# Five-stage software pipeline over 16 groups: every engine walks the groups in flight in another order

## Reference

```
# layer 0
x  = x + tanh(g_xattn[0]) * performer(q=LN(x), k=ctx, v=ctx)  # exp features, 16 heads of 8, causal prefix sums, num/den
x  = x + tanh(g_ffn[0])   * (sigmoid(xr @ Wr.T) * (relu(xk @ Wk.T)**2 @ Wv.T))   # xr, xk: mix of LN(x) and its previous row
# layer 1
x  = x + tanh(g_xattn[1]) * proj(att_w * softmax(S2) @ v + (1 - att_w) * softmax(q k.T) @ v)   # S2 from a gated softmax
x  = x + tanh(g_ffn[1])   * bitlinear(silu(bitlinear(LN(x), w_gate)) * bitlinear(LN(x), w_up), w_down)  # 8-bit rows, 3-level weights
```

## Time and profile before

| | us |
|---|---|
| median of 3 runs | 536.93 (536.85 to 537.79) |
| the profiled execution, its own time | 536.82 |
| its span in the trace | 535.0 |
| PE busy | 445.9 (83%) |
| DVE busy | 415.1 (78%) |
| ACT busy | 372.3 (70%) |
| POOL busy | 300.7 (56%) |

### The profile page before, as it was taken

How to read it: one execution, slowest core, us unless ns; L and a number is a source line. 1 busy time by engine, 2 the same in 40 slices (tenths; PEclk the granted TensorE clock), 3 DMA queues, 4 the chain that set the end, 5 groups by cost and what they waited for, 6 DMA issues and landing times.

```text
span 535.0 us, 18867 instructions
## 1 busy us (share of the span) xinstructions
PE 445.9 (83%) x7511; PEld 335.3 (63%) x7540; DVE 415.1 (78%) x1372; ACT 372.3 (70%) x769; POOL 300.7 (56%) x415
## 2 busy tenths in 40 slices
PE   0467588989999999999999999999999999877632
PEld 0355456767676767676868676767676767554521
DVE  3521368498989898998989898989898989898634
ACT  1423646587878787978787878787878787776532
POOL 4322035556666667575848584848485766563620
PEclk9999999899999999999999999999999999989765
DMA  7601010100101010101010101101010100000000
GB/s 169 146 2 37 6 32 11 34 9 2 46 10 45 9 45 10 43 12 42 11 42 13 40 15 29 26 20 35 10 42 3 50 4 22 2 21 12 2 10 11
DMA packets 35109, 15.14 MB, mean 28 GB/s; under 512 B 12496, under 2 KB 34896, under 8 KB 35024
## 3 DMA queue, kind: packets, MB, share of 16 engines
q1 hardware_dynamic: 32528, 12.79, 9.6%
q10 hardware_dynamic: 2496, 1.14, 0.9%
HBM read 9.73 MB, written 2.10 MB: 22 GB/s over the span
## 4 chain that ended last, share of the span: by engine, by line
PE 61%; ACT 13%; DVE 9%; POOL 8%; issue 5%; SPq 3%; DMA 1%; POOLq 0%
PE TP L1430 10%; PE MC L1463 8%; PE FP L1338 7%; PE MA L1354 6%; PE FP L1317 4%; POOL ft L385 3%; ACT ft L594 3%; ACT ft L595 3%; PE FP L1321 3%; PE FP L1319 3%; PE SP L1421 2%; ACT E L631 2%; PE SP L1534 2%; DVE WT L941 2%; PE FP L1280 2%
## 5 line engine op out<-in xcount | busy, mean ns | idle before, releaser
L1463 PEld LDWEIGHTS MC<-Vc,ET 128*64 128x64 f32 x2048 | 66.8, 140 | 28.0 <-issue 26.2
L385 POOL TENSOR_SCALAR ft<-ft 128x512 f32<-128x512 f32 x64 | 39.5, 617 | 74.2 <-ACT ft L595 70.6
L1463 PE MATMUL MC<-Vc,ET 128*64 128x25 f32 x2048 | 73.1, 220 | 3.2 <-ACT ET L636 2.3
L408 POOL TENSOR_TENSOR Zn<-E,rsh 128x1024 f32<-128x1024 f32 x32 | 60.9, 1902 | 11.3 <-DVE rsh L1001 11.1
L416 POOL TENSOR_TENSOR Zn<-Zn,Gs 128x1024 f32<-128x1024 f32 x32 | 60.8, 1902 | 3.1 <-DVE Gs L1012 1.6
L642 ACT ACTIVATE ET<-TP 128x512 f32<-128x512 f32 x64 | 38.0, 596 | 27.3 <-PE TP L1430 27.3
L941 DVE TENSOR_TENSOR WT<-FP,mask 128x512 f32<-128x512 f32 x64 | 43.4, 680 | 15.7 <-PE FP L1338 15.6
L1338 PE MATMUL FP<-ft 32*64 32x64 f32 x2048 | 39.6, 228 | 15.3 <-POOL ft L385 10.5
L1338 PEld LDWEIGHTS FP<-ft 32*64 32x64 f32 x2048 | 35.9, 141 | 23.3 <-issue 18.3
L981 DVE TENSOR_REDUCE mx<-SP 128x16 f32<-128x1024 f32 x32 | 39.0, 1219 | 6.6 <-PE SP L1421 6.5
L636 ACT ACTIVATE ET<-TP 128x512 f32<-128x512 f32 x64 | 38.0, 597 | 7.2 <-PE TP L1430 6.3
(11 more groups left out here) (195 smaller groups left out, 1158.4 us busy)
## 6 DMA issues: line engine op xcount, KB each, us to landing
Cd<-in_ctx SPq DMA_DIRECT2D x32, 128.0 KB, 2.9
kX<-kT SPq DMA_DIRECT2D x256, 8.0 KB
X<-in_x SPq DMA_DIRECT2D x16, 128.0 KB, 2.3
call<-in_ctx SPq DMA_DIRECT2D x4, 512.0 KB, 9.5
out_x<-X SPq DMA_DIRECT2D x16, 128.0 KB, 1.9
wffn<-in_L_ffn_w_gate ACTq DMA_DIRECT2D x1, 256.0 KB, 4.3
wffn<-in_L_ffn_w_up ACTq DMA_DIRECT2D x1, 256.0 KB, 4.7
wffn<-in_L_ffn_w_down ACTq DMA_DIRECT2D x1, 256.0 KB, 6.7
```

The costliest lines, as they stand in the source:

```text
L385: pool.tensor_scalar(f, f, EPS_K, 1.0, ALU.add, ALU.mult).then_inc(s("ftp"), 1)
L408: pool.tensor_tensor(z, E1[u][:, :].rearrange("p (h m) -> p h m", m=64), rsh[u][:, :].unsqueeze(2).to_broadcast([P, H, 64]), ALU.subtract) ...
L1463: last = mm(MC[64 * j:64 * j + 64, c + 32 * q:c + 32 * q + 25], weights[:, q, 64 * j:64 * j + 64], Vc[g.p][:, 2 * u + j, q, 0:25], start=T ...
```

## The change

No operation, buffer, bank or setup routine is added or removed. The order of the calls in `step` changes on POOL, ACT, DVE and PE, and waits are added or dropped where the new order asks for it. Some operations also move over a step's border: `least(c,0)`, `shift(c,0)`, `shifted(c,0)`, `ftp(a,1)`, `yD(d)` and `gates_mean(a)` are now at the end of the step before, `token_mix(c)` now stands at the start of the step after.

POOL's whole list, and the two helpers of DVE whose waits changed:

```diff
             def step(a, b, c, d, e):
-                if b:
-                    ftp(b, 1)
-                if d:
-                    shifted(d, 0)
                 if e:
                     quant_int(e)
+                if d:
+                    scaled(d, 0)
+                    shifted(d, 1)
+                    scaled(d, 1)
                 if c:
                     add_X2(c)
-                if d:
-                    scaled(d, 0)
                 if a:
                     veA(a)
+                    rsA(a)
...
+                if a:
+                    ftp(a, 1)
+                if c:
+                    shifted(c, 0)
...
             def gated_G(g, u):
 
-                if u == 0:
-                    at(v, s("r1"), g.k * 2 + 1)
+                at(v, s("r1"), g.k * 2 + 1 + u)
                 v.tensor_tensor(Gs[u][:, :], gate[g.p][:, u, :], rs1[u][:, :], ALU.mult).then_inc(s("Gs"), 1)
 
             def first(g, u):
 
-                if u == 1:
-                    at(v, s("r1"), g.k * 2 + 2)
                 v.scalar_tensor_tensor(n1[u][:, :, :], heads(MC[:, 0:256])[:, :, 0:8], wmix[:, 1:2],
```

More of the change, by code:

```diff
@@ L1124, in step @@
                 if d:
-                    shift(d, 1)
-                if c:
-                    ffn0(c)
+                    gated(d, 0)
+                    gated_G(d, 0)
+                    first(d, 0)
                 if b:
@@ L1130, in step @@
                 if d:
-                    gated_G(d, 0)
-                    first(d, 0)
+                    least(d, 1)
+                if e:
+                    quant_kh(e)
+                if d:
+                    shift(d, 1)
+                    gated(d, 1)
+                    gated_G(d, 1)
+                    first(d, 1)
                 if a:
                     stA(a)
-                if c:
-                    stC(c)
+                if e:
+                    ffn_h(e, 0)
+                    ffn_hu(e, 0)
                 if a:
@@ L1151, in step @@
                 if e:
-                    ffn_h(e, 0)
-                if d:
-                    gated(d, 1)
+                    ffn_hrec(e, 0)
+                    ffn_hs(e, 0)
+                if b:
+                    attend0(b)
                 if e:
[L1156 to L1161, removed]
+                    ffn_h(e, 1)
                 if c:
@@ L1214, in step @@
                     gates(a)
+                    gates_mean(a)
+                if d:
+                    stD(d)
+                    mvD(d)
+                if e:
+                    ffn_out(e, 0)
+                if c:
+                    least(c, 0)
+                if d:
+                    nbD(d)
                 if c:
@@ L1563, in step @@
             def step(a, b, c, d, e):
-                if d:
-                    outA(d, 0)
-                if c:
-                    ffn0_in(c)
                 if b:
@@ L1570, in step @@
                 if d:
+                    outA(d, 0)
                     turn1(d, 2)
+                    turn1(d, 3)
+                if c:
+                    ffn0_in(c)
+                if e:
+                    ffn_in(e)
+                if d:
+                    outA(d, 1)
+                if e:
+                    ffn_gu(e, 0)
+                if d:
+                    turn2(d, 0)
+                    turn2(d, 1)
+                if b:
+                    weights0(b, 1)
                 if c:
@@ L1574, in step @@
                 if d:
-                    turn1(d, 3)
+                    outB(d, 0)
                 if e:
-                    ffn_in(e)
-                if c:
-                    gates_bc(c)
-                if b:
-                    weights0(b, 1)
-                if e:
-                    ffn_gu(e, 0)
-                if d:
-                    outA(d, 1)
-                    turn2(d, 0)
+                    ffn_gu(e, 1)
                 if b:
@@ L1638, in step @@
                     features(a, 1)
+                if c:
+                    scores(c, 1)
+                    turn1(c, 0)
+                if e:
+                    ffn_dn(e, 1)
+                if b:
+                    rows_BT(b)
+                if c:
+                    turn1(c, 1)
             run(pe, step, late)
```

234 lines of the change are left out of this document (90 added, 144 removed).

## The result

The kernel after takes 538.42 us (median of 20 runs, 536.90 to 540.98), the kernel before on the same chip 536.87 us (20 runs, 534.40 to 538.98). The ratio is 1.0036, its 95% interval 1.0020 to 1.0052: slower by 0.36%. Forecast were 538.7 us and slower. The profiled execution took 539.44 us, with a span of 537.7.

What follows compares the result with a forecast made beforehand. PE was taken to set the pace, DVE close behind. 109.2 before the full steps, 337.8 for twelve of 28.15 and 89.9 behind make 536.9 us of span, with 1.8 around it 538.7; range 523 to 552, this case alone 533 to 545.

Steps and rivals of the forecast that it cites:

- The hold: Full step, DVE: gated_G(d,1) starts 0.14 us too late behind POOL's shifted(d,1) and is held until POOL ends, 1.76 us.
- two cases 16 us apart: Full step: either POOL's shifted(d,1) or DVE's gated_G(d,1) gets the shared SBUF port first; decides between 539 and 523 us.
- Its price: Full step: held DVE work delays PE, step 28.15 us against 27.05 without the port; 0.7 of 1.76 lies in existing pauses.
- The floor: Full step of the new order by the hand pass, without the held port: 27.05 us, 0.5 less than before.
- The removed waits and the path: Step's border: more PE work behind features(a,1) shrinks the wait for ftp; 0.35 us remains at weights0, 0.4 at features(a,1).
- The fill: Ahead of the full steps: sums begin earlier, weights0 of step 2 starts at 61.4, full steps begin at 109.2 us.
- The drain: Behind the full steps: begins 2.2 us of PE work earlier in its step; together 89.9 us against 89.0.
- +2.2, -0.8, -2.6 and +0.5: Drain: begins 2.2 us of PE work earlier, shifted(c,0) 0.8 earlier, step 18 gains 2.6, step 19 waits 0.5.
- its term for step 19: Drain, ACT: in step 19 ffn_mid(e,0) waits behind ffn_scale(e,1), 0.5 us.
- `gated_G` first at the port: Rival, full steps: gated_G(d,1) gets in ahead of POOL's shifted(d,1); step 27.05 us, time 522.8; chance 0.12.
- Late keys: Rival, full steps: SP's copies into kX land late for scores; step 28.8 us, time 546; chance 0.07.
- The clock's fall: Rival, full steps: more idle PE lowers its clock; 559 us if every step falls once, 549 if half; chance 0.20.

Runs made afterwards that it cites:

- e5_first: Kernel after with one wait more: POOL starts shifted(d,1) only when DVE has done gated_G(d,1); 533.22 us, ratio 0.9891 to the kernel before.
- e1_psum: Kernel after with gated_G(d,1) reading its reciprocal from a copy in PSUM, written by one more reciprocal; 531.33 us, ratio 0.9869 to the kernel before.
- e2_late: Kernel after with gated_G(d,1) moved behind ffn_hu(e,0) and its wait for the reciprocal moved to first; 535.15 us, ratio 0.9939 to the kernel before.
- e3_swap: Kernel after with first(d,1) ahead of gated_G(d,1); 536.3 us, ratio 0.9968 to the kernel before.
- e4_stats: Kernel after with first(d,1) and the statistics of group a ahead of gated_G(d,1); 530.93 us, ratio 0.9848 to the kernel before.
- e6_mix: Kernel before with token_mix moved from DVE's last of a step to the first of its next step; 537.96 us, ratio 0.9995 to the kernel before.
- e7_yB: Kernel of e5_first with yB(b) behind features(a,1) on ACT and rows_BT(b) behind turn1(c,1) on PE; 536.18 us, ratio 0.9963 to the kernel before.
- e8_best: Kernel of e7_yB with ffn_mid(e,0) ahead of ffn_scale(e,1) in steps without a group a; 535.87 us, ratio 0.9967 to the kernel before.

## Why the prediction came out right, and where it didn't

*The parts.* Full steps from 109.2, twelve of 28.15, drain 89.9 were forecast; measured are 110.1, 28.00 and 91.6. The span came out 0.8 us above the forecast, from misses of +0.9, -1.8 and +1.7, so the sum is better than its terms. That the median lies within 0.3 us of the forecast is luck, and the sign is not free of it either: of the two terms of the full step one was too high and the other too low (below). With the hold at its measured price and all else as forecast the time would have been 538.7 - 12 x (1.10 - 0.68) = 533.7 us, faster than before; with the measured floor and the forecast price 541.6. The range of 533 to 545 is also narrower than its own terms (12 x 0.3 and 2 us in each ramp make 7.6 either way, 531 to 546).

*The hold: right in its numbers.* `gated_G(d,1)` starts at 6.20 after `weights0` (forecast 6.28), POOL's `shifted(d,1)` at 6.08 (6.14), and it takes 1.81 us (1.76). Which of two instructions 0.12 us apart gets in first decided between two cases 16 us apart; e5_first forced the other one. The rule cited from the Trainium skill, SBUF — State Buffer, section "Who interferes with whom", agrees with the trace on both its points here: the instruction stands until POOL's ends (1.81, 1.54, 1.14 us by how late it comes), and with one operand in PSUM it doesn't wait (0.17).

*Its price: the mechanism right, the size wrong.* The step "Some 0.7 us of the 1.76 lies in pauses that DVE had anyway" was mis-sized. The series measures 0.95 to 0.98. So the hold costs 27.97 - 27.29 = 0.68 us a step, and not 1.1. PE was late at one place only, `ffn_gu(e,1)`; the waits forecast at `out0(b,0)` and `out0(b,1)` did not come.

*The floor.* "With nothing else changed my pass gives a step of 27.05 us" is 0.25 too low. The tail that the prediction added up (ACT's queue 4.5 and `ftp` with handoffs 1.55, so 6.05) measures 6.09, in the kernel after and in e5_first alike. The miss lies ahead of it, where PE goes from piece to piece nearly without a break: 21.20 us to the end of `features(a,0)` in e5_first, where the hand pass had 27.05 - 6.05 = 21.0. The two misses have opposite signs, and so the full step came out only 0.15 to 0.18 off.

*The removed waits and the path: wrong.* "The wait for `ftp` shrinks" did not happen. PE waits 0.60 us at `weights0` in the kernel after and in e5_first, against 0.56 before and 0.35 in the hand pass, and 0.56 at `features(a,1)` against 0.4. In e5_first PE's idle time is 1.73 us a step, more than the 1.47 of before. The step is 0.25 us shorter than before since PE's busy time fell from 26.07 to 25.56 us; why it fell is not shown. And the prediction closes the held step over ACT's queue, `features(a,1)`, `ftp(a,1)` and `weights0`. That is the chain where nothing is held (e1_psum, e2_late), but the kernel after and e3_swap close theirs over `ftp(a,0)`, `rs_D` and `nb_D`, and from there over DVE alone. This is also what the slack is: without its 1.65 us of stall the loop over DVE would take 27.97 - 1.65 = 26.3 us (an estimate from these two rows), 0.97 less than the loop over `weights0`, and a stall shorter than that does not show. From the end of `features(a,0)` to the next `shift(c,0)` it is 6.72 us by that way and was 6.68 by the prediction's (6.05, 0.05 and 0.58); that the two are alike is luck too.

*The fill.* `weights0` of step 2 was forecast at 61.4 and started at 61.48, the matmul over the sums at 54.2 and came at 54.17; step 2 at 22.3 and took 22.17. Step 3 took 26.45 where 25.0 and 0.5 for the clock were allowed. With the clock at 1.00 throughout, e3_swap and e4_stats took 25.79 and 25.80 for it, so the 25.0 is what was too low, by about 0.8. e6_mix shows how the account must be read: `token_mix` alone gives nothing of it, since PE's queue held the matmul back.

*The drain.* Its 89.9 cannot be worked out again from the terms named: 89.0 with +2.2, -0.8, -2.6 and +0.5 is 88.3, and the four operations of POOL have no size. It took 1.7 us more than forecast, though its term for step 19 is 0.2 and not 0.5, so the rest missed by 2.0. Two windows of the kernel after, in step 17:

```profile
474.67:478.30 3.63, 3.63 (x16) 3.09 (x16) 3.17 (x10) 1.82 (x4) 3.44 (x4) 0.53 0.06 11
488.40:499.50 11.10, 8.83 (x48) 4.73 (x48) 7.91 (x18) 5.18 (x10) 2.72 (x5) 0.69 0.01 2
```

In the first, TensorE is at the lower of its levels. The same pieces took 1.98 us in step 16 (448.29 to 450.27), so 1.65 are lost there. That does not explain the 2.0, though: the drain of before, from which the forecast started, has such a fall in its step 17 as well:

```profile
477.62:481.04 3.42, 3.42 (x32) 2.26 (x30) 3.29 (x13) 2.18 (x5) 3.42 (x3) 0.50 0.07 12
```

Both drains have a granted clock of 0.81 as a whole. With more clock the new order's drain does come out under 89.9: e3_swap has the same pieces behind the same wait of 0.85 us at full clock, 1.98 us again (473.93 to 475.91), and its drain takes 88.83 us at 0.84, though `gated_G` is held there too (1.51 and 1.54 us). Over the eight profiles of the new order and its variants the drain took 88.8 to 92.2 us at clocks of 0.84 to 0.79. So the miss of 2.0 is no larger than what the clock moves, and at the clock of before the new drain is 2.6 us longer than the old one, where 0.9 was forecast. Which of the named terms failed stays open.

*The rivals.* `gated_G` first at the port: it did not happen in the full steps. Late keys: in no full step does PE wait as much as 0.1 us ahead of the scores. The clock's fall: the full steps are at 1.00 throughout; only the ramps fell.

## What to carry to other kernels

When an order is changed, look for pairs of instructions on DVE and POOL that come to start together, and not only at what each waits for: the same 16-column product took 0.18 us in one place and 1.81 in another. Where one stands in the way, a wait on the other engine can be repair enough: e5_first adds one, moves nothing, and is by its ratio 1.1% faster than the kernel before. Here the stall cost what it exceeded the slack by, so measure the slack with two or three lengths of the stall. When waits are compared between two windows, count the borders in each: a wait at the border counts twice in one that holds both. An operation moved out of one gap of a queue that loops lands in the next one (e7_yB), and a moved operation helps only if the queue that waits for it is free to go (e6_mix).

## What was unexpected in the hardware

*A fall of the clock is not settled by the wait ahead of it.* In step 2, which has no group d, the kernel after and e4_stats run the same instructions in the same order. In the kernel after, PE pauses 1.12 us, and `features(a,1)` follows at full clock:

```profile
79.33 0.70 PE L1297 MATMUL FP<-qcT,Rf 32*128 32x256 f32 x4 [1.12 <-ACT ft L591]
```

In e4_stats it pauses the same 1.12 us, and goes on at the lower level:

```profile
78.92 1.11 PE L1301 MATMUL FP<-qcT,Rf 32*128 32x256 f32 x4 [1.12 <-ACT ft L591]
```

From there to the next `weights0` it is 4.32 us in the one and 6.98 in the other. Steps 2 and 3 together took 48.6 us in the kernel after, 49.9 to 50.7 in e1 to e4 and e7_yB, and 52.9 in e5_first (granted clocks 0.88 and 0.86). The plainest pair is e7_yB and e8_best, which have the same order on every engine up to step 15: 50.36 and 52.95 us. One profile's ramp is therefore known to a few us only, more than the difference between the two kernels. Of the twelve full steps of a kernel 7 to 11 lie within 0.02 us of their median (the others are mostly up to 0.1 longer, a few more, once 0.9), and it is they that the experiments were read by. What decides whether the clock falls was not found.

*Who gets in first is decided within hundredths of a microsecond.* The same instruction of POOL, `quant_int` (`xq<-xm`), shows both cases. Started 0.015 us ahead of DVE's `shift` by the unrounded starts, it let it in: `shift` took its 0.17 us, and POOL's took 0.45 where it takes 0.41 in the other full steps. Started 0.025 us ahead of `gated_G(d,0)`, in step 4 of e3_swap (and in e4_stats likewise), it held it:

```profile
115.79 0.40 POOL L427 TENSOR_SCALAR xq<-xm 128x256 bf16<-128x256 f32 x1 [0.34 <-ACT xm L650]
115.82 0.40 DVE L1006 TENSOR_TENSOR Gs<-gate,rs 128x16 f32<-128x16 f32 x1
```

So the rival of the prediction that had `gated_G` in first rested on a lead of 0.015 us, and the 0.12 us of the kernel after are far on the other side.

*Not every operation of POOL holds DVE to its end.* In the kernel before, `gated_G(d,1)` of the step of the earlier trace rows starts at 289.32, 0.04 us into POOL's `rs_C<-ve_C,mhalf` (128x2, 289.28, 0.69 us long), which also reads SBUF, and lasts 0.18 us. By the rule of the Trainium skill cited above it would have stood for 0.65; the measurement decides, and what sets this operation apart was not tried.
